# Cross-attention 1 of a Flamingo megakernel: the keys' high part written by ScalarE at once, their rest by VectorE in quarters; GpSimd's order in cross-attention 0 rewritten

## The reference

```python
x = x + jnp.tanh(g_xattn[0]) * _L0_xattn_ref(_layernorm(x), ctx_2048, mask)       # softmax(x ctx^T / sqrt(512)) ctx, 1601 keys per batch
x = x + jnp.tanh(g_ffn[0]) * _L0_ffn_ref(_layernorm(x), w_up, w_down)             # Hadamard transform, 8 bit tokens, ternary weights, relu^2
x = x + jnp.tanh(g_xattn[1]) * _L1_xattn_ref(_layernorm(x), ctx_2048)
x = x + jnp.tanh(g_ffn[1]) * _L1_ffn_ref(_layernorm(x), weight1, weight2, weight3) # SwiGLU with NF4 round trip of the weights

# _L1_xattn_ref(qkv, y), per group of 32 channels:
q = qkv.reshape(bs * N_HEADS, ch, length)
k = v = y.reshape(bs * N_HEADS, ch, -1)
weight = jnp.einsum('bct,bcs->bts', q * scale, k * scale)
weight = jax.nn.softmax(weight.astype(jnp.float32), axis=-1).astype(weight.dtype)
a = jnp.einsum('bts,bcs->bct', weight, v)
```

## Time and profile before

| what | value |
|---|---|
| median of 3 runs | 1832.2 us (1830.99 to 1832.41) |
| profiled execution | 1832.33 us, of which the span of the trace is 1830.5 us |
| mean granted PE clock | 0.951 |
| busy over the span | PE 88%, DVE 65%, ACT 46%, POOL 45% |
| stage A, B, C, D | 0 to 468.9, to 701, to 1546, to 1830.5 us |

### The profile page before, as it was taken

How to read it: one execution, slowest core, us unless ns; L and a number is a source line. 1 busy time by engine, 2 the same in 40 slices (tenths; PEclk the granted TensorE clock), 3 DMA queues, 4 the chain that set the end, 5 groups by cost and what they waited for, 6 DMA issues and landing times. The chain is left out here.

```text
span 1830.5 us, 22118 instructions
## 1 busy us (share of the span) xinstructions
PE 1610.6 (88%) x7540; PEld 614.6 (34%) x7568; DVE 1184.1 (65%) x1538; ACT 841.9 (46%) x1241; POOL 826.7 (45%) x324
## 2 busy tenths in 40 slices
PE   5999999799688886789999999899999996889898
PEld 2444444344334441122222222222222221444443
DVE  3769999887355556677767777677777641443443
ACT  1321221212334442477777777677777775111110
POOL 0022214643112222767778777687777777000000
PEclk9999999899889996799999999999999999899999
DMA  9232223023211113312222222222222241000000
GB/s 325 76 121 78 84 83 106 30 95 119 75 32 26 27 27 93 113 41 59 67 63 72 76 75 75 76 75 51 55 67 67 54 109 32 1 23 0 23 23 23
DMA packets 136395, 124.36 MB, mean 68 GB/s; under 512 B 61774, under 2 KB 112226, under 8 KB 136294
## 3 DMA queue, kind: packets, MB, share of 16 engines
q1 hardware_dynamic: 131302, 112.56, 21.7%
q10 hardware_dynamic: 4992, 10.49, 1.7%
HBM read 73.49 MB, written 10.76 MB: 46 GB/s over the span
## 5 line engine op out<-in xcount | busy, mean ns | idle before, releaser
L1477 ACT ACTIVATE c_prob<-c_scores,ctx_scales 128x512 f32<-128x512 f32 (+1 forms) x832 | 531.0, 684 | 221.1 <-PE c_scores L1533 218.0
L1384 DVE TENSOR_REDUCE c_piece_max<-c_unit 128x1 f32<-128x804 f32 x512 | 488.3, 987 | 208.5 <-PE c_unit L1516 205.2
L1322 POOL TENSOR_TENSOR c_prob_sum<-c_prob_sum,c_prob 128x2048 f32<-128x2048 f32 x96 | 434.8, 4529 | 90.9 <-ACT c_prob L1477 86.9
L1533 PE MATMUL c_scores<-c_queries,c_keys 97*128 97x512 f16 (+1 forms) x832 | 321.4, 392 | 40.6 <-ACT c_prob L1477 33.2
L1516 PE MATMUL c_unit<-c_khigh,c_qdiag 128*128 128x402 f16 x1024 | 274.2, 351 | 44.6 <-DVE c_piece_max L1384 32.7
L1542 PE MATMUL c_out<-c_prob,c_VT 128*32 128x512 f32 (+1 forms) x1664 | 225.0, 613 | 0.1
L1533 PEld LDWEIGHTS c_scores<-c_queries,c_keys 97*128 97x128 f16 (+1 forms) x832 | 80.9, 98 | 369.7 <-ACT c_prob L1477 322.6
L676 PE MATMUL a_S<-a_ctxT,a_xnT 128*128 128x401 f32 x512 | 190.2, 516 | 7.2 <-ACT a_prob L633 3.9
L706 PE MATMUL a_o<-a_ctx,a_probT 128*128 128x512 f32 (+1 forms) x416 | 183.2, 597 | 0.0
L1516 PEld LDWEIGHTS c_unit<-c_khigh,c_qdiag 128*128 128x128 f16 x1024 | 90.5, 100 | 152.5 <-DVE c_piece_max L1384 90.2
L567 ACT COPY a_probT<-a_tp 128x512 f32<-128x512 f32 x48 | 28.0, 585 | 217.8 <-PE a_tp L691 210.8
(11 more groups left out here) (197 smaller groups left out, 1905.8 us busy)
## 6 DMA issues: line engine op xcount, KB each, us to landing
c_k<-in_keys SPq DMA_DIRECT2D x16, 801.0 KB, 6.7
c_keys<-c_khigh SPq DMA_DIRECT2D x128, 100.1 KB, 2.2
a_ctx<-in_ctx SPq DMA_DIRECT2D x12, 1024.0 KB, 7.2
c_VT<-in_values SPq DMA_DIRECT2D x16, 768.0 KB
a_ctxT<-in_ctxT SPq DMA_DIRECT2D x12, 802.0 KB, 4.7
c_keys<-c_krest SPq DMA_DIRECT2D x64, 100.1 KB, 2.2
a_weights<-in_L_ffn_weight SPq DMA_DIRECT2D x3, 1408.0 KB, 14.4
weights_back<-a_weights SPq DMA_DIRECT2D x3, 1408.0 KB, 8.3
```

Source lines behind the costliest of these rows:

```text
L1322: nc.gpsimd.tensor_tensor(psum4[:], a[:], prob[(j * MC + c) % RING][:], ALU.add).then_inc(sums_taken, 2 if i == 1 else 1)
L1384: nc.vector.tensor_reduce(piece_max[j % 2][:, k // 2, k % 2:k % 2 + 1], U[bank(unit)][:, :, 0:PIECE], axis=AX.XY, op=ALU.max).then_inc(uni ...
L1477: nc.scalar.activation(prob[(j * MC + c) % RING][0:w, h, :], STp[h % 2][0:w, :], ACT.Exp, scale=score_scale[0:w]).then_inc(exp_done, 1)
L1533: nc.tensor.matmul(STp[h % 2][0:w, :], K[p][:, h, c * P:c * P + w], Q[p][:, h, :], start=True, stop=True).then_inc(scores_ready, 1)
```

## The change

In stage A the maximum of the context is taken in quarters of the columns, 16 in all, each waiting only for its own quarter's load, and the next load of a quarter waits only for that quarter. Where the bites and quarters stand in the iterations is a table now (`BITES_AT`, `TOPS_AT`); the last three bites are in iteration 15, where all were done by iteration 14 before. GpSimd's order is written out. In stage B the last batch's `scale` of the next tile stands ahead of `quantize` of the one before. In stage C, for all groups but the first two, ACT writes `khigh` straight from the unscaled f32 keys with the scale in the instruction, in two halves after the exponentials of c=2 and c=3; the keys are no longer scaled in place. The rest `krest` is computed by DVE (key times scale minus khigh, one instruction) in four pieces of 400 to 402 columns after units 17, 20, 23 and 26, where GpSimd did it at the end of the slot.

```diff
-        BITES_FROM, BITES_EACH = 3, 4
+        BITES_AT = {3: 4, 4: 3, 5: 4, 6: 3, 7: 4, 8: 4, 9: 4, 10: 3, 11: 4, 12: 4, 13: 4, 14: 4, 15: 3}
+        TOPS_AT = {0: [0, 1], 1: [2], 3: [3]}
+        for b in range(1, B):
+            TOPS_AT.update({4 * b: [4 * b, 4 * b + 1], 4 * b + 1: [4 * b + 2, 4 * b + 3]})
...
-                if b > 0:
-                    sp.wait_ge(ctx_topped, b)
                 for n in range(4):
                     if b > 0:
+                        sp.wait_ge(ctx_topped, (b - 1) * 4 + n + 1)
...
-            for n in range(N):
-                if n + 1 < N:
-                    scale(n + 1)
-                if n in (1, 3):
-                    normalize(2 + n // 2)
-                weigh(n)
-                if n > 1:
-                    for m in range(2 * n - 4, 2 * n - 2):
-                        clip_bits(m)
+            scale(1)
+            weigh(0)
+            scale(2)
+            normalize(2)
+            weigh(1)
+            scale(3)
+            clip_bits(0)
+            weigh(2)
+            scale(4)
+            clip_bits(1)
+            normalize(3)
+            clip_bits(2)
+            weigh(3)
+            scale(5)
+            clip_bits(3)
+            clip_bits(4)
+            weigh(4)
+            clip_bits(5)
+            clip_bits(6)
+            weigh(5)
+            clip_bits(7)
...
-            def context_top(b):
-                for n in range(4):
-                    dve.wait_ge(ctxT_loaded[n], 16 * (b + 1))
-                nc.vector.tensor_reduce(ctx_tops[:, b:b + 1], CT[:], axis=AX.XY, op=ALU.max, apply_absolute_value=True).then_inc(ctx_topped, 1)
-                if b == B - 1:
-                    dve.wait_ge(ctx_topped, B)
-                    nc.vector.tensor_reduce(ctx_tops[:, B:B + 1], ctx_tops[:, 0:B], axis=AX.X, op=ALU.max).then_inc(ctx_topped, 1)
+            def context_top(i):
+                b, n = divmod(i, 4)
+                dve.wait_ge(ctxT_loaded[n], 16 * (b + 1))
+                nc.vector.tensor_reduce(ctx_tops[:, i:i + 1], CT[:, :, n * PIECE:(n + 1) * PIECE], axis=AX.XY, op=ALU.max,
+                                        apply_absolute_value=True).then_inc(ctx_topped, 1)
...
-                if k % ST == 2:
-                    context_top(k // ST)
                 if k == 1:
                     block_maxima()
                     layernorm(1)
+                for i in TOPS_AT.get(k, []):
+                    context_top(i)
...
-                if k >= BITES_FROM:
-                    for _ in range(BITES_EACH):
-                        if bites:
-                            bite(*bites.pop(0))
+                for _ in range(BITES_AT.get(k, 0)):
+                    bite(*bites.pop(0))
+            assert not bites
             add_out(K - 2)
             context_scales()
-            for n, m in bites:
-                bite(n, m)
             add_out(K - 1)
...
+                alone = v is not None and v[0] == 2 and v[1] == B - 1
+                if pending is not None and not alone:
                     quantize(pending)
                     pending = None
                 if v is not None and v[0] in (0, 2):
                     scale(v)
+                    if pending is not None:
+                        quantize(pending)
                     pending = v
...
-        PARTS = 4
+        PARTS, RESTS, RESTS_AT = 4, 4, (17, 20, 23, 26)
...
-                    sp.wait_ge(krest_ready, n + 1)
+                    if isinstance(n, int) and n < 2:
+                        sp.wait_ge(first_krest_ready, n + 1)
+                    else:
+                        sp.wait_ge(krest_ready, n + 1)
...
-                pool.wait_ge(khigh_ready, n + 1)
+                pool.wait_ge(khigh_ready, 2 * (n + 1))
                 wait(pool, stacked, (n - 1) * STACKS)
-                nc.gpsimd.tensor_tensor(krest[j][:], kt[j][:], khigh[j][:], ALU.subtract).then_inc(krest_ready, 1)
+                nc.gpsimd.tensor_tensor(krest[j][:], kt[j][:], khigh[j][:], ALU.subtract).then_inc(first_krest_ready, 1)
...
                     rest_of_q(g + 2, j % 2)
-                    rest_of_k(g + 2, j % 2)
...
+            def rest_of_keys(n, j, i):
+                cols = slice(i * MK // RESTS // 2 * 2, (i + 1) * MK // RESTS // 2 * 2)
+                if i == 0:
+                    dve.wait_ge(khigh_ready, 2 * (n + 1))
+                    dve.wait_ge(stacked, (n - 1) * STACKS)
+                if i == RESTS - 1:
+                    dve.wait_ge(krest_begun, (RESTS - 1) * (n - 1))
+                nc.vector.scalar_tensor_tensor(krest[j][:, cols], kt[j][:, cols], key_scale, khigh[j][:, cols],
+                                               ALU.mult, ALU.subtract).then_inc(krest_ready if i == RESTS - 1 else krest_begun, 1)
...
+                    if main and more and u in RESTS_AT:
+                        rest_of_keys(g + 2, j % 2, RESTS_AT.index(u))
...
-            def split_keys(n, j):
+            def split_first_keys(n, j):
                 act.wait_ge(k_loaded[j], turn(n, j))
-                if not isinstance(n, int) or n > 1:
+                nc.scalar.activation(kt[j][:], kt[j][:], ACT.Copy, scale=key_scale).then_inc(kscaled, 1)
+                act.wait_ge(kscaled, n + 1)
+                nc.scalar.copy(khigh[j][:], kt[j][:]).then_inc(khigh_ready, 2)
+
+            def split_keys(n, j, half):
+                cols = slice(half * MK // 2, (half + 1) * MK // 2)
+                if half == 0:
+                    act.wait_ge(k_loaded[j], turn(n, j))
                     act.wait_ge(unit_full, FULL0 + place(n - 2, PAIRS - 1) + 1)
                     act.wait_ge(stacked, (n - 1) * STACKS)
-                nc.scalar.activation(kt[j][:], kt[j][:], ACT.Copy, scale=key_scale).then_inc(kscaled, 1)
-                act.wait_ge(kscaled, n + 1)
-                nc.scalar.copy(khigh[j][:], kt[j][:]).then_inc(khigh_ready, 1)
+                nc.scalar.activation(khigh[j][:, cols], kt[j][:, cols], ACT.Copy, scale=key_scale).then_inc(khigh_ready, 1)
...
-                    if c == 2 and more:
-                        split_keys(g + 2, j % 2)
+                    if c in (2, 3) and more:
+                        split_keys(g + 2, j % 2, c - 2)
...
-                    pe.wait_ge(khigh_ready, n + 1)
+                    pe.wait_ge(khigh_ready, 2 * (n + 1))
```

More of the change, by code:

```diff
@@ L129, in cross_attention_0 @@
         wtops_all = sb("a_wtops_all", [P, P, 4])
-        ctx_tops = sb("a_ctx_tops", [P, B + 1])
+        ctx_tops = sb("a_ctx_tops", [P, 4 * B + 1])
         BIT_PIECES = 4
@@ L311, in _ @@
                     sp.dma_start(wtops_all[:], flat_tops.rearrange("(o r) k -> o r k", o=1).broadcast_to([P, P, 4])).then_inc(wtops_loaded, 16)
-            sp.wait_ge(ctx_topped, B + 1)
-            sp.dma_start(flat_ctx_top.rearrange("(p o) -> p o", o=1), ctx_tops[:, B:B + 1]).then_inc(ctx_top_out, 16)
+            sp.wait_ge(ctx_topped, 4 * B + 1)
+            sp.dma_start(flat_ctx_top.rearrange("(p o) -> p o", o=1), ctx_tops[:, 4 * B:4 * B + 1]).then_inc(ctx_top_out, 16)
             sp.wait_ge(ctx_top_out, 16)
@@ L473, in bit_scales @@
                 nc.vector.reciprocal(bit_recip[:], shared["bit_scales"][:]).then_inc(bit_scales_ready, 1)
-            def context_top(b):
-                for n in range(4):
-                    dve.wait_ge(ctxT_loaded[n], 16 * (b + 1))
-                nc.vector.tensor_reduce(ctx_tops[:, b:b + 1], CT[:], axis=AX.XY, op=ALU.max, apply_absolute_value=True).then_inc(ctx_topped, 1)
-                if b == B - 1:
-                    dve.wait_ge(ctx_topped, B)
-                    nc.vector.tensor_reduce(ctx_tops[:, B:B + 1], ctx_tops[:, 0:B], axis=AX.X, op=ALU.max).then_inc(ctx_topped, 1)
+            def context_top(i):
[3 more added lines that the diff above has]
+                                        apply_absolute_value=True).then_inc(ctx_topped, 1)
+                if i == 4 * B - 1:
+                    dve.wait_ge(ctx_topped, 4 * B)
+                    nc.vector.tensor_reduce(ctx_tops[:, 4 * B:4 * B + 1], ctx_tops[:, 0:4 * B], axis=AX.X, op=ALU.max).then_inc(ctx_topped, 1)
             def context_scales():
@@ L946, in _ @@
                     rest(u)
-                if pending is not None:
+                alone = v is not None and v[0] == 2 and v[1] == B - 1
+                if pending is not None and not alone:
                     quantize(pending)
@@ L1150, in cross_attention_1 @@
         qrest_ready = sem("c_qrest_ready")
+        first_krest_ready = sem("c_first_krest_ready")
+        krest_begun = sem("c_krest_begun")
         krest_ready = sem("c_krest_ready")
@@ L1361, in _ @@
             dve.sem_inc(unit_read, UNITS0)
+            dve.sem_inc(krest_ready, 2)
             def moments_begun(n):
@@ L1479, in _ @@
             split_queries(0, 0)
-            split_keys(0, 0)
+            split_first_keys(0, 0)
             def slot(g, j, main, nxt, more, later):
@@ L1484, in slot @@
                     split_queries(1, 1)
```

(2 more changed lines are left out.)

## The result

The changed kernel takes 1897.4 us (median of 4 runs, 1896.9 to 1905.6) against 1832.3 (4 runs, 1831.0 to 1833.8): the ratio is 1.0363, 95% interval 1.0336 to 1.039. It is slower by 65 us. The forecast of 1814 was wrong, and so was the range, which ended at 1870; the measured time lies in the place of the rival that I had called full hold, 1886 to 1899. The profiled execution is the slowest of the four, 1905.55 us with a span of 1903.7, so sums over the trace are made against its 1905.55 - 1832.33 = 73.2 us.

The account below looks back on a forecast made before the run. Stages A and C were taken to run at PE's pace, so only PE's idle time could be won; C -13.5, A -2.5 and B -2 made -18 us against 1832.33, giving 1814, range 1784 to 1870.

Parts of the forecast that it names:

- full hold: Stage C rival, chance 0.20: rests wait until GpSimd's add_up ends, slots 6.4 us longer less 1.86; 1886, up to 1899.
- GpSimd's hold as a price per input element: GpSimd holds DVE while it reads, 0.82 ns per input element; add_up in stage C holds 3.36 of 4.52 us.
- the sum for stage C: Rests add 1.2 us per slot, the vanished wait gives 1.86; with g=0 and the slow matmuls, -13.5 us.
- g=0: First slot of stage C: PE's wait for the exponential goes, -0.9 us.
- the slow matmuls: Stage C: five of thirteen slots longer by 1.56 us, some 8 us in all; half taken as gone, -4.
- A: Stage A: waits for GpSimd's clips go, DVE's ledger and the tail take most back; -2.5 us.
- B: Stage B: the last batch's second-tile scale no longer stands behind quantize's wait; -2 us, 0 to -2.5.
- ACT's halves: Stage C: ACT's 3.16 us in a row become two pieces over half the columns, 0.9 us each.
- the rest alone: Stage C: one rest of 400 columns on DVE takes about 0.57 us, with 0.4 and 0.8 as ends.
- PE's wait for the exponential: Stage C: the score product's wait goes, -1.86 us in each of 13 slots.
- 7.5 us there: Stage A: the maximum of k=10 comes 15 us late, so PE stands still for about 7.5 us.

Follow-up runs that it names:

- a_only: Stage A of the changed kernel alone, all else from the kernel before; 1828.8 us, ratio 0.9971 to the kernel before.
- rests_at_end: Changed kernel with the four rests on VectorE moved to after units 29, 30, 31 and 32, at the slot's end; 1852.2 us.
- end_diag: rests_at_end with the next queries' diagonal DMAs issued after the second head's stacking instead of behind all stacking DMAs and loads; 1791.4 us.
- one_input: Changed kernel with each rest on VectorE a one-input scaling of the keys, high part not subtracted (output differs); 1892.7 us.
- pool_one_input: Changed kernel with GpSimd's sums two to seven one-input copies of half the columns, a tiny addition ahead of each (output differs); 1789.1 us.
- gpsimd_diag: Changed kernel with the rest back on GpSimd, ACT scaling keys in place in halves after c=4 and c=5, diagonal DMAs issued earlier; 1788.8 us.

## Why the prediction was wrong

**The step that failed** is GpSimd's hold as a price per input element. I had made 0.82 ns per element out of two rows of different kinds: a clip with one input that held for 0.84 of its 3.32 us, and a two-input instruction that held nearly to its end. One number fitted both, and for the add_up it gave 3.36 of 4.52 us. It fitted because both holds were counted from the moment at which VectorE's operation was asked for, while the sum for stage C lets the hold begin with GpSimd's instruction (987.07 + 3.36). Counted in that way, the same rows give 289.29 + 6.33 - 1.62 - 288.58 = 5.42 us of 5.57 for the two-input instruction, 0.96 ns per input element, and 276.98 + 2.46 - 1.62 - 276.38 = 1.44 us for the clip, 1.41 ns: no one price fits. The trace of the kernel before has more of the two-input kind, such as this bite, which takes 0.88 us alone, and GpSimd beside it:

```profile
223.27 5.47 DVE L433 TENSOR_SCALAR a_neg<-a_weights 128x2816 bf16<-128x2816 bf16 x1
```
```profile
223.09 4.91 POOL L354 TENSOR_TENSOR a_weights<-a_weights,a_srecip 128x2816 bf16<-128x2816 bf16 x1
```

It was let go at 227.86, 0.14 us before GpSimd's end at 228.00, and the bite of the earlier trace rows 0.15 us before. So the full hold could be read before the change was run. The runs showed two kinds of behaviour in the price's place: beside a GpSimd instruction with two inputs VectorE stands still until that one ends, whether it is 2.36 or 4.52 us long; beside a copy with one input it ran on. The numbers laid out for the full hold then came true one by one: first rest 3.2 us (3.16 to 3.23), second 4.8 (4.66 to 4.80), 6.4 us of stops per slot (2.37 + 4.27 = 6.6). The difference between 3.36 and 4.52 decided because the second rest, asked for after unit 20, fell behind the start of the next add_up instead of ahead of it, by 0.14 to 0.27 us in the thirteen slots.

**Its sum.** 13 slots: 724.96 us between the take_outs of g=0 and g=13 (1533.71 - 808.75), against 651.87 before, so +73.1, or 5.6 each. The two windows, before and after, and PE's waits in them, before (two lines) and after:

```profile
808.51:1460.38 651.87, 600.15 (x3539) 166.33 (x3539) 461.38 (x532) 492.94 (x742) 510.35 (x179) 0.98 0.25 67
```
```profile
808.75:1533.71 724.96, 635.43 (x3539) 170.23 (x3539) 580.15 (x584) 477.06 (x742) 481.75 (x166) 0.93 0.23 61
```
```profile
PE c_scores L1533 <- ACT c_prob L1477: 24.2, 13, 1.9
PE c_unit L1516 <- DVE c_piece_max L1384: 24.1, 91, 0.5
```
```profile
PE c_unit L1553 <- DVE c_piece_max L1404: 85.9, 91, 4.3
```

Per slot that is +4.8 of waits for the maxima (6.6 for the two stops, less 1.9 of short waits that they took the place of), -1.9 for the exponential, and +2.7 of slower matmuls: PE is busy 35.3 us longer with the same 3539 products. The full hold as I had priced it, 4.5 per slot, had the slow matmuls only in its upper end. g=0: +5.6 (two of its rests are held, 2.33 and 3.23 us), where I had -0.9. A and B: -5.4. Together +73.3 of 73.2.

**What was right.** ACT's halves last 0.96 us (0.9 forecast), the rest alone 0.62 (0.57), and PE's wait for the exponential is gone. In A the waits for GpSimd's clips are gone, and in their place PE waits 6.7 us for the exponential at the tile where the two GpSimd instructions in a row hold the bites:

```profile
308.32 5.25 PE L688 MATMUL a_S<-a_ctxT,a_xnT 128*128 128x401 f32 x8 [6.71 <-ACT a_prob L645]
```

I had 7.5 us there. VectorE's two operations beside them each took 5.6 us where they take 0.9 alone. A came out at -1.6 (-2.5 forecast); a_only, 3.7 us faster than the kernel before by its medians and 1.4 by its trace, agrees in kind. B was mis-sized, -3.8 us where I had -2.

**What I had not priced** was SyncE's queue. In the change it didn't matter, as the rests were ready early; but it bounds every kernel here whose rest comes late in the slot, and it was worth 61 us between rests_at_end and end_diag (1852.2 - 1791.4): 37.5 us of waits, and slower matmuls for the rest. The slow matmuls were undersized in the forecast as well. I had counted five long slots and 8 us, and took 4 of it; seven slots before lasted over 50 us, and between the kernel before and end_diag PE's busy time in the thirteen slots falls by 10.8 us (600.15 to 589.38).

**The weight given.** The full hold had 0.20. The two-input row of stage A spoke for it; the clip alone spoke against it, and the clip is not the form that runs in stage C. The rule of the Trainium skill that I weighed ("SBUF — State Buffer", section "Who interferes with whom") gave the right case: by it the second of two such instructions blocks for all of the first's. The traces agree beside the additions (4.80, 2.60, 0.99 us for an operation of 0.62), and differ beside the one-input copy, where the operation took 0.63 us. The same section counts VectorE's tensor_scalar among the operations that can take the shared port and tensor_reduce among those that never do; the held scaling of one_input (4.6 us instead of 0.42) and the maxima, 0.99 us beside an add_up, agree with that, though the maxima here read PSUM.

## What to carry to other kernels

Before moving work to VectorE, look at what GpSimd does at that moment: beside a two-input elementwise instruction of GpSimd a short VectorE operation on SBUF lasts until that one ends, and then a 0.6 us piece costs 5 us. The same four pieces in GpSimd's idle time, with the queue mended, are within 3 us of the kernel that has none of them on VectorE (1791.4 against 1788.8). Take the price from the row whose form is that of the neighbour you will have, and don't fit one formula through rows of different forms. When a producer moves later, follow the queue that it heads to its last member: 24 DMA issues of 0.63 us stood between a rest and a transfer that had nothing to do with it.

## What the runs showed of the hardware

- GpSimd's two-input f32 additions of 2048 and of 1024 elements held VectorE's operations from SBUF nearly to their own end: a two-input operation of 0.62 us ended 0.42 to 0.44 us behind the addition's end, whether it was asked for 0.14 or 3.7 us behind its start. A one-input scaling from f32 to f16 (0.42 us alone) was held in the same way; it ended 0.22 to 0.24 us behind and took up to 4.6 us. Beside a one-input copy of 1024 elements the two-input operation took 0.63 us when it was asked for 1.57 us or more behind the copy's start.
- Beside the one-input clips of stage A in the kernel before, no bite was more than 0.85 us late. Those asked for 0.60 to 1.30 us behind a clip's start were 0.71 to 0.85 us late, those asked for 1.45 to 2.95 us behind it were not, and two of those asked for in a clip's last microsecond were (0.72 and 0.83 us).
- VectorE's maxima out of PSUM were not held: 0.99 us each beside the add_ups as without them.
- The hold acts the other way too: in the changed kernel GpSimd's L1329 took 1.59 to 1.61 us in the thirteen slots, behind a held rest, where it takes 1.26 to 1.28; in pool_one_input a copy took 3.11 us instead of 2.77 where a rest began 0.14 us ahead of it.
- PE's stops cost more than their length: without them (end_diag, gpsimd_diag) a slot ran at a granted clock of 1.00, the upper of the two levels (2.4 GHz); in the changed kernel the two slots shown had 0.94.
